# Ten matmuls of the identity in each of two edge loops of a graph network on one Trainium2 core

## The reference

```python
# layer 0: attention over edges, 6250 nodes, 100000 edges sorted by dst, D=128, 8 heads of 16
scores = einsum('ehd,ehd->eh', q[dst], k[src]) / sqrt(16)
ex = exp(scores - segment_max(scores, dst)[dst])
alpha = ex / (segment_sum(ex, dst)[dst] + 1e-9)
emb = segment_sum(alpha[:, :, None] * v[src], dst).reshape(N, D) @ W0
h1 = layer_norm(X + emb);  x = LN(X + layer_norm(h1 + relu(h1 @ fc1 + b) @ fc2 + b))
# layer 1: two directions, each on half of the edges
h_dir = segment_sum(relu(concat(x[src], edge_attr, req) @ W1 + b1) @ W2 + b2, dst)
out = LN(x + relu(((1 + eps) * x + h_in + h_out) @ Wu + bu))
```

## Time and profile before

| | |
|---|---|
| time, median of 3 runs | 2725.98 us (2723.42 to 2731.78) |
| the profiled execution, its own time | 2717.23 us |
| its span, first to last instruction | 2715.2 us |
| PE busy / PEld busy | 1557.6 us (57%) / 1227.2 us (45%) |
| DVE, ACT busy | 1442.3 us (53%), 748.1 us (28%) |
| POOL busy | 1592.9 us (59%) |
| mean granted TensorE clock | 0.719 of full |
| bytes moved | 251.96 MB, 93 GB/s |

### The profile page before, as it was taken

One profiled execution on the slowest core, in us unless ns is written; L12 is line 12 of the kernel. 1 busy time (PEld: TensorE's weight loads), 2 busy tenths in 40 slices (PEclk: granted clock), 3 DMA queues, 4 the chain that ended last, 5 costly groups with the idle time before them and its releaser, 6 DMA issues.

```text
span 2715.2 us, 32144 instructions
## 1 busy us (share of the span) xinstructions
PE 1557.6 (57%) x7355; PEld 1227.2 (45%) x7356; DVE 1442.3 (53%) x2972; ACT 748.1 (28%) x1512; POOL 1592.9 (59%) x1662
## 2 busy tenths in 40 slices
PE   6354565556555555556786354556465565654656
PEld 4244455545545554455664233344343443433434
DVE  5265666666666666666575134345254353443535
ACT  3333333333433333333574011111111111111111
POOL 3665666666666666662532756665656656656661
PEclk9567767767777676767898566677677776767767
DMA  7554444444444444442011211221211212211221
GB/s 250 146 172 140 141 135 133 132 145 133 133 129 146 133 133 129 146 133 76 18 42 44 54 47 51 51 57 49 54 50 50 58 51 52 55 51 50 54 54 28
DMA packets 148256, 251.96 MB, mean 93 GB/s; under 512 B 74681, under 2 KB 99401, under 8 KB 147179
## 3 DMA queue, kind: packets, MB, share of 16 engines
q0 software_dynamic: 64048, 156.29, 20.2%
q1 hardware_dynamic: 83612, 94.45, 11.3%
q10 hardware_dynamic: 560, 0.82, 0.1%
HBM read 229.88 MB, written 21.54 MB: 93 GB/s over the span
## 4 chain that ended last, share of the span: by engine, by line
issue 29%; PE 25%; another core or an unknown queue 19%; DVE 15%; DVEq 5%; ACT 3%; DMA 2%; POOL 0%; SPq 0%; ACTq 0%; PEldq 0%; POOLq 0%
PE ps L1102 10%; PE ps L1078 8%; DVE arena L1626 4%; DVE arena L1635 2%; DVEq L1655 2%; DVE arena L1499 1%; ACT arena L880 1%; DVEq L1654 1%; PE ps L1029 1%; DMA arena<-d 1%; PE ps L1119 1%; DVEq L1652 1%; DVE arena L1445 1%; DVE arena L1554 1%
## 5 line engine op out<-in xcount | busy, mean ns | idle before, releaser
L670 POOL DMA_INDIRECT arena<-kvq_tab,arena x784 | 748.1, 954 | 455.7 <-issue 249.2
L727 POOL DMA_INDIRECT arena<-y_tab,arena x784 | 742.6, 947 | 447.5 <-issue 229.1
L1252 PEld LDWEIGHTS ps<-arena 128*128 128x128 f32 x1568 | 294.5, 255 | 407.5 <-issue 376.6
L1252 PE MATMUL ps<-arena 128*128 128x128 f32 x1568 | 319.1, 346 | 268.4 <-issue 250.9
L1102 PE MATMUL ps<-arena 128*128 128x136 f32 x1568 | 322.0, 393 | 245.7 <-issue 132.3
L1102 PEld LDWEIGHTS ps<-arena 128*128 128x128 f32 x1568 | 312.4, 297 | 268.2 <-issue 268.2
L957 ACT ACTIVATE arena<-arena 128x512 f32<-128x512 f32 x224 | 119.4, 569 | 800.1 <-DVE arena L1635 504.8
L1078 PE MATMUL ps<-arena 128*128 128x128 f32 x1596 | 286.7, 350 | 72.1 <-issue 32.3
L1239 PE MATMUL ps<-w1blk,eaT 113*128 x456 | 284.9, 709 | 64.8 <-issue 64.2
L1078 PEld LDWEIGHTS ps<-arena 128*128 128x128 f32 x1596 | 265.9, 258 | 98.4 <-issue 98.4
L1445 DVE TENSOR_TENSOR arena<-ps,arena 128x512 f32<-128x512 f32 x224 | 136.9, 611 | 320.8 <-remote 316.0
(11 more groups left out here) (258 smaller groups left out, 1973.1 us busy)
## 6 DMA issues: line engine op xcount, KB each, us to landing
arena<-d SPq DMA_DIRECT2D x59, 897.0 KB
arena<-kvq_tab,arena POOLq DMA_INDIRECT x784
arena<-y_tab,arena POOLq DMA_INDIRECT x784
kvq_tab<-arena SPq DMA_DIRECT2D x7, 1344.0 KB, 7.0
arena<-in_edge_attr_dram SPq DMA_DIRECT2D x60, 112.0 KB
y_tab<-arena SPq DMA_DIRECT2D x10, 625.0 KB
arena<-kvq_tab SPq DMA_DIRECT2D x59, 64.0 KB
out_dram<-arena SPq DMA_DIRECT2D x56, 64.0 KB
```

Source lines behind the costliest of these rows:

```text
L670: g.indirect_dma_start(kv_s[:, r, t, :], None, kvq_tab.rearrange("n (a d) -> (n a) d", a=3), bass.IndirectOffsetOnAxis(ap=v3(idx, RING)[:, ...
L727: g.indirect_dma_start(yg_s[:, r, t, :], None, y_tab, bass.IndirectOffsetOnAxis(ap=v3(idx1, RING)[:, r, t:t + 1], axis=0)).then_inc(m_g[r] ...
L1252: last = mm(bank(6 + u)[:, 0:W], yg_s[:, r, t, :], hot1_s[:, u, t, :], start=(t == 0), stop=(t == G - 1))
```

## The change

A helper `keep_running` issues `KEEP` = 10 matmuls of the identity by the identity (128 x 128, float32) on TensorE into a given place of PSUM. Nobody reads what they write, and they signal nothing. In the first loop it stands ahead of the sums, behind the wait for `l_cur` (the place in bank 5 is the sums' own, which that wait makes free); the wait for `l_hot` is moved behind it. In the second loop it stands behind the final product, in passes that have a new chunk, and writes to columns of bank 6 or 7 that nothing else uses.

```diff
+KEEP = 10
...
+            def keep_running(to):
+
+                for _ in range(KEEP):
+                    mm(to, ident[:, :], ident[:, :])
...
                 if b_ is not None:
-                    pe.wait_ge(l_hot, minus2)
                     if c_ is not None:
                         pe.wait_ge(l_cur, minus3)
+                        keep_running(bank(5)[:, 0:P])
+                    pe.wait_ge(l_hot, minus2)
                     pe.wait_ge(l_pva, minus2)
...
                     mm(to, dbu[:, :], deg[0:2, ds(base, W)], start=False, stop=True).then_inc(f_o, 1)
+                    if new is not None:
+                        keep_running(bank(6 + w)[:, 2 * W:3 * W])
```

## The result

| | before | after |
|---|---|---|
| median on one chip | 2724.7 us (4 runs) | 2824.3 us (4 runs, 2822.1 to 2830.7) |
| ratio | | 1.0355, 95% interval 1.0327 to 1.0384 |
| profiled execution, span | 2715.2 us | 2820.1 us |
| mean granted clock | 0.719 | 0.762 |

What follows compares the result with a forecast made beforehand. It took the gathers' own time plus a pause every turn, ended by TensorE's held-up signals, as the bound. 2717.2 + 119 (first loop) + 66 (second) = 2902; the runs' median lies 8.8 higher: 2910 us, range 2800 to 3080.

Steps and rivals of the forecast that it cites:

- the store: Both loops: a place between TensorE and the rest takes some 118 instructions (102 in second loop), emptied only when gathers pause.
- resumption: Both loops: the first gather on GpSimd behind a pause, from which the prediction counted TensorE's instructions.
- the crawl: Both loops: the stretch in which TensorE starts an instruction only every 1.4 us or so.
- Rival B: Both loops: crawl starts by time or something other than TensorE's instructions; the ten fill idle time, 2726 us; chance 0.15.
- A: Rival: clock pays, sums on the path gain 130 us in first loop, 2596; weaker form 2696; chance 0.09 with it.
- the first loop's 2.2 us a turn: First loop: release of TensorE's signals to resumption grows from 1.0 to 3.2 us; over 54 pauses 119 us.
- 29 + 118 + 17 + 5 = 169: First-loop turn: 29 instructions before the resumption, 118 + 17 from there to the crawl, 5 in it; turn has 170.
- the second loop's 1.3 us a chunk: Second loop: longer pauses from 40 more instructions a chunk, +1.3 us for 51 chunks, 66 us; ends 0 and 4.4.
- double turns: Second loop: turns of two chunks, 42.10 us with 28 gathers and no pause between; if they stay, pauses grow up to 2 us.
- With more register instructions between: Second loop: the reason given for the store taking 102 instructions there instead of some 118.
- C: Rival, both loops: the ten at half clock hold up sums and next chunk by 0.4 us; 42 us, 2768; chance 0.10.
- D: Rival, both loops: full price, nothing given back, 4.4 x 105 = 462 us, 3188; chance 0.05.

Runs made afterwards that it cites:

- The wide version: The changed kernel with first-loop matmuls only, as three of 512, 512 and 256 columns (12 instructions for 40), against the kernel before: ratio 1.0018.

## Why the prediction came out as it did

**Right: what paces the loops.** Gathers take their own time, and what changes is the pause between them. The 105 us of span lie in the two loops, where the forecast put them, except for 16. That TensorE's signals stay in altogether while gathers are issued is too strong: with half of the sums' matmuls one came out between two gathers.

**Right: the store and its count.** From a resumption to the crawl 113, 117 and 115 instructions went here and with one-column matmuls, in 9.0 to 11.4 us, against 112 to 119 in 14.1 to 15.1 before. Rival B (a start by time) falls by this and by the price itself; that it is instructions, not columns, is shown by the wide and the narrow matmuls, and that register additions do not count, by their run. The fixed number is the one behind the first 3 us, 87 to 92 in the medians of the first loop; the 118 holds only as long as about 30 go ahead of it. The prediction's own sum had this (118 + 17, and 102 + 12 in the second loop, where the median after the change is 115), while its list of signs says 118 and 102.

**Open: what the store is.** The runs show how many instructions go and which kinds count, not where they pile up. Besides a place between TensorE and the rest, it could belong to the recording of the profile: the loads and products that count are instructions that it records, the register additions are not in its counts (32144 instructions with them and without), and every execution here has a recorded span and clock. No run without recording is there to tell.

**Right: the clock buys nothing.** The sums fell from 393 to 290 ns a product, and the turn did not care. The wide version shows it alone: the clock kept up at no price, and no gain (A). The Trainium skill, "TensorE: Matmul & The Clock Gate", section "HAM oscillation — how this bites in real kernels", says that a wait between TensorE's bursts puts it back to the low clock, so that the next burst starts slow. On the clock the rows agree, 381 ns a product with one-column matmuls in the hole and 292 with wide ones. The time would follow only where the matmuls that get faster are on the path, and here they lie under the gathers.

**Wrong in size: the first loop's 2.2 us a turn (119 us; measured 54.6).** The step that failed is the sum 29 + 118 + 17 + 5 = 169, which sends all 170 instructions of a turn through one pause. GpSimd waits ahead of pieces 1, 2 and 3, but the prediction let only the first of these waits act. With the crawl early, the queries are late too, the wait ahead of piece 2 stops GpSimd once more, and that pause empties the store a second time. A turn with the extra pause takes 22.1 us (299.33 to 321.47) or more, the next one the old 21.05, and the mean is 1.0 us over before. Without that wait the turn is the one forecast (22.9 and 23.2 us for 23), and the loop costs 104 us. So the sum was right for the pause that it knew.

**Wrong in size: the second loop's 1.3 us a chunk (66 us; measured 34, 0.66 a chunk).** The working gave +0.8 for single turns without double ones, and I added 0.5 in case double turns stayed. None stayed; +0.8 x 51 = 41 was the better figure.

**Wrong: why the second loop's count is smaller.** "With more register instructions between" falls by the register additions. Counted from 3 us behind a resumption, up to the crawl, the kernel before has 90 and 86 in the first loop, and 74 and 87 in the two stretches of the second; over the loops the medians are 88 and 84, against 115 and 102 from the resumption. So about half of the difference is what goes in those first 3 us (median 27 against 20). The rest stays open.

**Missing: 11.3 us behind the last gather, and 4.2 ahead of the first.** TensorE's timeline behind the last gather (2666.5 before, 2760.1 after). Before:

```profile
2679.96 0.31 PE L1273 MATMUL ps<-ident,arena 128*128 128x128 f32 x1 [1.56 <-DVE arena L1671]
...
2702.47 0.30 PE L1273 MATMUL ps<-ident,arena 128*128 128x128 f32 x1 [0.60 <-DVE arena L1671]
```

After:

```profile
2773.11 0.30 PE L1282 MATMUL ps<-ident,arena 128*128 128x128 f32 x1 [0.69 <-DVE arena L1680]
...
2806.88 0.28 PE L1282 MATMUL ps<-ident,arena 128*128 128x128 f32 x1
```

Before, L1273 comes at 2679.96, 2691.24 and 2702.47; after, L1282 at 2773.11, 2784.35, 2795.64 and 2806.88. Passes without gathers are as long as before (11.2 us; the ten, 2.5 us at full clock, are hidden in them), but there is one more of them: TensorE is one chunk further behind when the gathers end. More instructions are not the only way to this: with half of the sums' matmuls the stretch is 60.9 us and has the extra pass too. The start's 4.2 us look like scatter: the first gather comes between 67.4 and 71.8 us in the twelve profiles, at 68.2 with twenty matmuls.

**The order of the cases.** The measured 2824 lies nearer to C's 2768 than to the forecast's 2910, near the lower end of the range from 2800. But C's mechanism is not what the runs show: it has the ten hold up the sums at half clock, and the sums got faster. The two loops were forecast at 185 us and cost 89; the 16 us outside them, which the forecast put at nothing, brought the total a little nearer by luck. D (462 us) is reached by nothing here: even the second ten cost 281.

## What to carry to other kernels

Where software gathers run back to back, count the instructions of the engine that feeds the next wait, not its microseconds: the same columns in 12 instructions were free, in 40 cost 2%. And when a change makes a signal late, go through every wait for it on the engine that paces: one that never ended last can take over, and shorten the loop (35 us here) or lengthen it. Look also at what an engine still has to do when its loop's bound ends: a backlog of one pass is paid in full.

## What the runs showed of the hardware

- While indirect gathers are issued 1.25 us apart, TensorE gets some 115 loads and products out in the first loop, at whatever rate, and then one in about 1.4 us, until the gathers stop. Those of the first 3 us behind a pause come on top: without them it is 87 to 92, also where none go there. Matmuls of one column count like those of 128; register additions do not count.
- A gap of 2.1 us between two gathers (ahead of 304.89) is enough for another 117 instructions without a crawl, though 76 had gone since 299.33.
- Signals of TensorE come late while gathers are issued: in most turns only when GpSimd has stopped, and in 24 chunks of the run with fewer matmuls early enough that GpSimd did not stop for the sums (once seen some 7 us behind them, between two gathers).
- The price of more instructions is far from linear: 92 to 97 us per ten matmuls up to ten, 281 for the next ten, and with 28 instructions fewer than the kernel before has, 12 us come back.
